# An adaLN-conditioned mixture-of-experts block on one core: loads, casts and splits at the start are put in another order

## What is computed

```python
# conditioning: one linear map plus a low-rank (rank 16) adapter chosen per sequence
A, Bm = lora_As[itok], lora_Bs[itok]                 # slot of each sequence, 32 slots
xt = x @ W.T + b + 2.0 * ((x @ A) @ Bm)
# router: 16 experts in 4 groups, 2 groups kept, 2 experts taken per token
scores = softmax(xt @ router_w + router_b) + router_bias
gate = top2_of_best_2_groups(scores)
# experts (512 -> 128 -> 512), and a shared expert (512 -> 256 -> 512)
y = sum_e gate[:, e] * ((silu(xt @ ew1[e] + eb1[e]) * (xt @ ew2[e] + eb2[e])) @ ew3[e] + eb3[e])
z = (silu(xt @ sw1 + sb1) * (xt @ sw2 + sb2)) @ sw3 + sb3
out = x + y + z
```

## Time and profile before

| | us |
|---|---|
| median of 3 runs | 132.3 |
| the runs | 130.42, 249.07, 132.3 |
| profiled execution | 131.28 |
| span of the profiled execution | 129.5 |

### The profile page before, as it was taken

The page is one execution under the profiler, slowest core; times in us unless marked ns, Lnnn a source line. Parts: engine busy times, 40 slices in busy tenths (PEclk is TensorE's granted clock), DMA queues, the critical chain, the costliest instruction groups (busy, mean ns, idle before and its releaser), DMA issues.

```text
span 129.5 us, 2241 instructions
## 1 busy us (share of the span) xinstructions
PE 123.5 (95%) x815; PEld 102.3 (79%) x815; DVE 86.0 (66%) x194; ACT 48.3 (37%) x85; POOL 19.8 (15%) x33
## 2 busy tenths in 40 slices
PE   6999996999996999999999999999999999999991
PEld 6988874987885777888888889987788888888891
DVE  1496095497469718989999984355906279997731
ACT  1780373595559516203963574441022110000000
POOL 7374025000000020000027200033620000000000
PEclk9999999999999999999999999999999999999999
DMA  4999888659999699989305899402426999422222
GB/s 102 375 287 347 259 331 273 225 199 370 317 301 309 140 178 175 321 305 358 123 0 116 321 309 384 161 11 83 162 86 209 328 369 375 179 97 109 110 94 81
DMA packets 16908, 28.77 MB, mean 222 GB/s; under 512 B 1952, under 2 KB 6432, under 8 KB 16768
## 3 DMA queue, kind: packets, MB, share of 16 engines
q1 hardware_dynamic: 11728, 17.07, 40.5%
q10 hardware_dynamic: 3952, 7.34, 16.5%
q0 software_dynamic: 1216, 4.20, 10.3%
HBM read 19.17 MB, written 9.44 MB: 221 GB/s over the span
## 4 chain that ended last, share of the span: by engine, by line
PE 77%; DMA 9%; DVE 5%; ACT 3%; issue 2%; SPq 2%; DVEq 0%; ACTq 0%
PE bank L993 58%; DMA xT_raw<-in_xT 9%; PE bank L1192 6%; PE bank L1206 3%; PE bank L1049 2%; ACT xT_h L462 2%; PE bank L1267 1%; PE bank L1060 1%; PE bank L1037 1%; PE bank L1182 1%; SPq L319 1%; DVE sw_l L682 1%; ACT loraA_sb L472 1%; PE bank L1023 1%; PE bank L1097 1%
## 5 line engine op out<-in xcount | busy, mean ns | idle before, releaser
L993 PE MATMUL bank<-xtT_h,sw_h 128*128 128x512 f32 x32 | 12.9, 405 | 1.2 <-DVE sw_l L682 1.2
L993 PE MATMUL bank<-xtT_h,w12e_h 128*128 128x512 f32 x32 | 13.1, 409 | 0.0
L993 PE MATMUL bank<-xtT_h,w12e_l 128*128 128x512 f32 x32 | 12.5, 391 | 0.0
L993 PE MATMUL bank<-xtT_l,w12e_h 128*128 128x512 f32 x32 | 12.5, 391 | 0.0
L993 PE MATMUL bank<-xtT_h,sw_l 128*128 128x512 f32 x32 | 12.5, 390 | 0.0
L993 PE MATMUL bank<-xtT_l,sw_h 128*128 128x512 f32 x32 | 12.5, 390 | 0.0
L966 DVE SCALAR_TENSOR_TENSOR x_sb<-rows_sb,val,x_sb 128x512 f32<-128x512 f32 x16 | 11.7, 748 | 0.2
L972 DVE TENSOR_TENSOR x_sb<-x_sb,bank 128x512 f32<-128x512 f32 (+1 forms) x9 | 5.6, 626 | 4.8 <-PE bank L993 4.8
L682 DVE TENSOR_TENSOR xT_l<-xT_raw,xT_h 128x512 fp32r<-128x512 f32 (+1 forms) x6 | 5.2, 867 | 4.5 <-ACT xT_h L462 4.5
L993 PEld LDWEIGHTS bank<-xtT_h,sw_h 128*128 128x128 f32 x32 | 6.0, 188 | 2.8 <-DVE sw_l L682 1.4
L790 DVE SCALAR_TENSOR_TENSOR heT_sb<-bank,b_dense,sg_sb 128x512 f32<-128x512 f32 x4 | 3.0, 751 | 7.7 <-PE bank L993 7.7
(11 more groups left out here) (184 smaller groups left out, 294.1 us busy)
## 6 DMA issues: line engine op xcount, KB each, us to landing
y_rows<-zeros ACTq DMA_DIRECT2D x2, 2048.0 KB, 12.2
rows_sb<-y_rows SPq DMA_DIRECT2D x8, 512.0 KB, 8.4
xT_raw<-in_xT SPq DMA_DIRECT2D x8, 256.0 KB, 5.8
xt_rows<-xt_turned SPq DMA_DIRECT2D x8, 256.0 KB, 8.1
x_sb<-in_x SPq DMA_DIRECT2D x1, 2048.0 KB, 11.2
w_ring<-in_w_turned SPq DMA_DIRECT2D x4, 512.0 KB, 9.0
out<-x_sb ACTq DMA_DIRECT2D x7, 256.0 KB, 2.0
condW_raw<-in_condWT ACTq DMA_DIRECT2D x4, 256.0 KB, 4.5
```

Of the source, the lines that this page charges most:

```text
L993: mm = pe.matmul(out, a[p], b[q], start=(start and n == 0), stop=(stop and n == 2))
```

## The change

x's second half is issued right behind the first, ahead of the six small loads, and the shared weights behind them without the wait for the second lora gather. VectorE casts the first chunk of x (a new semaphore, `first_hi`; the counts of `xT_hi` move by one). ScalarE does `copy_loraA(1)` ahead of `hi_lhT(0)`, both halves of `sw12` ahead of `hi_lhT(2)`, and `copy_loraA(3)` ahead of `hi_loraB(3)`. On VectorE the slot arithmetic comes behind the cast, both rests of x's second half come ahead of the lora rests, `lo_sw12(1)` comes ahead of `lo_lora(3)` and of the first choice, and the four transposes of the first half, which were interleaved with its rests, are done two by two: behind `lo_sw12(0)` and behind `choose(0)`. A wait for `xt_ready` stands before the transposes of the second half.

```diff
@@ -225,7 +225,7 @@
         xT_hi, xT_done, sw12_hi, sw12_done = sem("xT_hi"), sem("xT_done"), sem("sw12_hi"), sem("sw12_done")
         loraA_copied, xt_whole, loraB_hi, loraB_done = (
             sem("loraA_copied"), sem("xt_whole"), sem("loraB_hi"), sem("loraB_done"))
-        zeros_ready = sem("zeros_ready")
+        first_hi, zeros_ready = sem("first_hi"), sem("zeros_ready")
         lhT_hi, lhT_done, xtT_hi, xtT_done = sem("lhT_hi"), sem("lhT_done"), sem("xtT_hi"), sem("xtT_done")
         pool_step, consts_ready = sem("pool_step"), sem("consts_ready")
         lora_row_ready = sem("lora_row_ready")
@@ -322,16 +322,14 @@
             sp.dma_start(slot_i[:], seq_slot).then_inc(seq_in, 16)
             for k in range(1, KC):
                 load_xT(0, k)
+            for k in range(KC):
+                load_xT(1, k)
             sp.dma_start(condb_sb[:], cond_b).then_inc(small_in, 16)
             sp.dma_start(rw_sb[:], router_w).then_inc(small_in, 16)
             sp.dma_start(rb_col[:], router_b).then_inc(small_in, 16)
             sp.dma_start(rbias_sb[:], router_bias.partition_broadcast(P)).then_inc(small_in, 16)
             sp.dma_start(sb12_sb[:], sb12).then_inc(small_in, 16)
             sp.dma_start(b12_sb[:], b12).then_inc(small_in, 16)
-            sp.wait_ge(xT_in[KC - 1], 16)
-            for k in range(KC):
-                load_xT(1, k)
-            sp.wait_ge(lora_in[1], 16)
             sp.dma_start(sw12_raw[:], sw12).then_inc(sw12_in, 16)
             sp.dma_start(sw3_raw[:], sw3).then_inc(sw3_in, 16)
             sp.dma_start(b3s_raw[:], b3s).then_inc(b3s_in, 16)
@@ -509,14 +507,15 @@
                 act.dma_start(condW_raw[:, k, :], condWT[k]).then_inc(condW_in[k], 16)
             for k in range(KC):
                 hi_condW(k)
-                hi_xT(0, k, k + 1)
+                if k >= 1:
+                    hi_xT(0, k, k + 1)
             hi_xT(1, 0, 2)
+            hi_xT(1, 2, 4)
             hi_loraB(0)
             copy_loraA(0)
-            hi_xT(1, 2, 4)
             hi_loraB(1)
+            copy_loraA(1)
             hi_lhT(0)
-            copy_loraA(1)
             hi_lhT(1)
             act.wait_ge(small_in, 16 * 6)
             for m in range(KC):
@@ -530,13 +529,13 @@
             hi_loraB(2)
             copy_loraA(2)
             hi_sw12(0)
+            hi_sw12(1)
             hi_lhT(2)
-            hi_loraB(3)
             copy_lgT(0)
             copy_loraA(3)
+            hi_loraB(3)
             exps(0)
             hi_lhT(3)
-            hi_sw12(1)
             for m in range(KC):
                 whole_xtT(1, m)
             for m in range(KC):
@@ -672,11 +671,6 @@
             dve.wait_ge(consts_ready, 3)
             then(dve.tensor_scalar(part16_i[:], part_i[:], RANK - 1, None, ALU.bitwise_and))
             then(dve.tensor_copy(part16[:], part16_i[:]))
-            dve.wait_ge(seq_in, 16)
-            then(dve.tensor_copy(slot_f[:], slot_i[:]))
-            then(dve.tensor_scalar(slot_f2[:], slot_f[:], float(RANK), None, ALU.mult))
-            dve.tensor_scalar(lora_row[:], slot_f2[:], part16[:, 0:1], None, ALU.add).then_inc(lora_row_ready, 1)
-
             def rest(lo, whole, hi, made_sem):
 
                 dve.tensor_tensor(lo, whole, hi.bitcast(F32), ALU.subtract).then_inc(made_sem, 1)
@@ -687,7 +681,10 @@
 
             def lo_xT(n, first, last):
                 hi, lo = xT_split[n]
-                dve.wait_ge(xT_hi, last if n == 0 else KC + last // 2)
+                if n == 0 and first == 0:
+                    dve.wait_ge(first_hi, 1)
+                else:
+                    dve.wait_ge(xT_hi, first if n == 0 else KC - 1 + last // 2)
                 rest(lo[:, first:last], xT_raw[n][:, first:last], hi[:, first:last], xT_done)
 
             def lo_lora(g):
@@ -749,6 +746,12 @@
                                        cols_i[:, 0:E].unsqueeze(1).unsqueeze(1).to_broadcast(by_pick), ALU.is_equal))
                 dve.tensor_tensor(chosen[:, tiles], sel[:, 0, tiles], sel[:, 1, tiles], ALU.add).then_inc(chosen_ready, 1)
 
+            dve.wait_ge(xT_in[0], 16)
+            dve.tensor_copy(xT_split[0][0][:, 0, :], xT_raw[0][:, 0, :]).then_inc(first_hi, 1)
+            dve.wait_ge(seq_in, 16)
+            then(dve.tensor_copy(slot_f[:], slot_i[:]))
+            then(dve.tensor_scalar(slot_f2[:], slot_f[:], float(RANK), None, ALU.mult))
+            dve.tensor_scalar(lora_row[:], slot_f2[:], part16[:, 0:1], None, ALU.add).then_inc(lora_row_ready, 1)
             for k in range(KC):
                 lo_condW(k)
                 lo_xT(0, k, k + 1)
@@ -759,25 +762,29 @@
             then(dve.tensor_scalar(slot_no_pad[:], slot_no[:], float(K * T + T), None, ALU.add))
             then(dve.tensor_scalar(row_no[:], part_i[:], 63, None, ALU.bitwise_and))
             lo_xT(1, 0, 2)
+            lo_xT(1, 2, 4)
             lo_lora(0)
-            lo_xT(1, 2, 4)
             lo_lora(1)
             dve.wait_ge(consts_ready, 5)
             mask_lh(0)
             mask_lh(1)
             for m in range(KC):
-                turn_xt(0, m)
                 lo_xtT(0, m)
             lo_lora(2)
             lo_sw12(0)
+            turn_xt(0, 0)
+            turn_xt(0, 1)
             mask_lh(2)
+            lo_sw12(1)
             lo_lora(3)
             dve.wait_ge(small_in, 16 * 6)
             shift_logits(0)
             mask_lh(3)
             choose(0)
-            lo_sw12(1)
+            turn_xt(0, 2)
+            turn_xt(0, 3)
             dve.wait_ge(lgT_done, 1)
+            dve.wait_ge(xt_ready, KC)
             for m in range(KC):
                 turn_xt(1, m)
 
@@ -1002,7 +1009,10 @@
                         pe.matmul(cond_bank(0, m)[:], w[:, m * P:(m + 1) * P], x, start=start, stop=False)
 
                 pe.wait_ge(condW_hi, k + 1)
-                pe.wait_ge(xT_hi, k + 1)
+                if k == 0:
+                    pe.wait_ge(first_hi, 1)
+                else:
+                    pe.wait_ge(xT_hi, k)
                 over_dims(w_hi, x_hi, k == 0)
                 pe.wait_ge(condW_done, k + 1)
                 over_dims(w_lo, x_hi, False)
```

## The result

| | before | after |
|---|---|---|
| median of the runs timed together, us | 131.5 | 135.15 (134.28 to 135.75) |
| profiled execution, us | 131.28 | 135.57 |
| its span, us | 129.5 | 133.7 |

The changed kernel takes 1.030 times the time of the kernel before, 95% interval 1.017 to 1.043. The forecast was 131.9 with a range of 129.2 to 133.6, so the kernel is slower than forecast and outside the range.

What follows compares the result with a forecast made beforehand. TensorE, busy 95%, was taken as the bound. It gains 2.0 us by the shared experts, then stands 2.7 us for late dense weights; with + 0.6 net, 131.28 + 0.6 = 131.9 us, range 129.2 to 133.6.

Steps and rivals of the forecast that it cites:

- The early part: Up to the shared experts: waits of 1.1 and 1.2 us vanish, TensorE 2.0 us ahead; failing had 7%, 133.0 us.
- the new wait of 0.4 for the fourth mask's rest: Before the shared experts: TensorE, arriving earlier, waits about 0.4 us for VectorE's mask rest, between 0 and 0.7.
- VectorE's cast of x's first chunk: At the start: taken as 0.61 us from ScalarE's row, bounds nothing to twice that; gain 0.1 us, between 0 and 0.2.
- The step on x's second half: Loads at the start: issuing it early does not slow the first half and only frees VectorE, whose mask stood at 19.80.
- The queue: SP's queue before the dense experts: late stores delay the weights, TensorE stands 2.7 us, net + 0.6 us; 62%.
- The rival that they would run faster and the gain stay: First half's late stores: faster draining keeps the gain in whole or good part, 128.8 to 130.5 us; 18%.
- The rule of the Trainium skill, "DMA: Bandwidth & Descriptors", Specifications: Stores: 512-byte pieces suffice for line rate, so the 2.0 us gain would stay; the prediction preferred the trace's 184 GB/s.
- The rival of slower stores: Before the dense experts: eight stores drain under 160 GB/s, first weights land after 65.0, 133.9 us and up; 8%.
- The clock: After the 2.7 us standstill: TensorE falls to 1.2 GHz level, costing 2.0 us, 133.9 in all; a rival at 5%.
- the likeliest case: The dense weights' delay takes back the early gain, 130.8 to 133.2 us for 10% in the stores' rate; 62%.
- The late gather: Lora gathers come late beside the shared weights, early gains are lost, stores leave 1.1 us later: 133.0 us; 7%.
- The 3.9 us of slack: Second lora gather: landed at 14.21, turned at 18.07, so sharing DMA with the shared weights was priced at 0.

Runs made afterwards that it cites:

- E10: The changed kernel run again with nothing altered; 134.21 us, 1.026 times the kernel before.
- E8: E3 with x's second half issued behind the small loads, once the first half has landed, as before the change; 129.77 us, 0.992 times the kernel before.
- E2: The changed kernel, but SP again waits for the second lora gather before issuing the shared weights; 134.57 us, 1.032 times the kernel before.
- E4: The kernel before with only the first half's transposes moved late, plus the `xt_ready` wait; 135.75 us, 1.033 times the kernel before.
- E1: The changed kernel with the first half's four transposes put back between the splits; 128.86 us, 0.987 times the kernel before.
- E3: The changed kernel with transposes early again and shared weights again waiting for the second lora gather; 128.34 us, 0.982 times the kernel before.
- E6: The changed kernel, transposes still late, with x's 2 MB load moved behind the routed blocks' weights; 128.57 us, 0.985 times the kernel before.
- E7: E3 with x's 2 MB load moved behind the routed blocks' weights; 128.57 us, 0.981 times the kernel before.
- E9: E1 with the shared weights' loads issued ahead of the small loads; 128.94 us, 0.984 times the kernel before.
- E5: The changed kernel with six filler identity products on TensorE ahead of the dense weights' wait; median 133.33 us (131.82 to 134.51), no ratio.

## Why the prediction was wrong, by its own steps

**The early part: right, and a little small.** Both waits went. The terms of the sum were to come to 2.0 at the shared experts; in E10 the first shared matmul came at 39.67 against 42.04, so 2.4. The difference is the new wait of 0.4 for the fourth mask's rest, which none of the profiles shows: that term should have been 0. VectorE's cast of x's first chunk took 0.43 us (0.61 was taken). The step on x's second half was incomplete: "it only frees VectorE" overlooked ScalarE, whose first copy would otherwise stand behind that half's casts (E8, 1.2 to 1.4 us).

**The queue: right, nearly to the number.** The forecast beside E10, the execution without the late gather:

| step | forecast us | E10 us |
|---|---|---|
| stores of the first half issued | 41.4 | 41.24 |
| x landed | 61.75 | 50.02 + 11.5 = 61.5 |
| first dense weights cast (forecast: landed) | 63.05 | 62.89 |
| first dense matmul | 67.35 | 67.24 |
| standstill before it | 2.7 | 2.94 |

So the price of the late stores, taken from 184 GB/s in the earlier trace rows, held. The rival that they would run faster and the gain stay is answered by these times. The rule of the Trainium skill, "DMA: Bandwidth & Descriptors", Specifications, was set against that row; these runs bear the row out. The rival of slower stores is answered too: the weights came before 65.0 even in the profiled execution with the late gather (64.76).

**The clock: this step failed.** The prediction worked out a standstill of 2.7 us, said that none of that length is in the trace, and then went on as if the chip answered it like the ones of 1.1 and 1.2 that are there. It gave the other answer 5%, with a price of 2.0 us. Behind every standstill of 2.7 to 3.3 us that came without filling products (changed kernel, E2, E4, E10) the clock went to 0.50; the price was 1.7 us in three of them, 2.8 in E2. With the predicted 0.6 that makes 2.3, and 131.8 - 129.5 = 2.3 is what E10's span shows. These executions were no exceptions: in all 16 runs of the four kernels the mean granted clock was 0.974 to 0.987, in E1's four 0.998 or more. The prediction's own line for this case was 133.9; the medians are 134.2 and 135.15. The rule of the Trainium skill, "TensorE: Matmul & The Clock Gate", Part 1, that idleness sets the engine to half clock, stood beside that rival, and these traces agree with it (0.50). The chance was the error, not the mechanism: the likeliest case and this rival were one chain, since the first made the second's condition, and it should have been the likeliest or near it.

**The late gather: right as a rival, in one execution.** The 3.9 us of slack were exceeded in the first profile (second turn at 19.76, against 18.07 in the earlier trace rows), and the stores left at 42.92 instead of 41.24. The 1.9 us by which that span exceeds E10's are about this. How often the gather is late in runs without a profile can't be read, so it is not shown that it accounts for the 0.9 us between the two medians. The runs' mean clocks offer another reason: 0.974 or 0.975 in three of the first four, in one of E10's four, and that one took 1.1 us more than the mean of E10's others.

**The sum of it.** The change is two changes. All but the moved transposes make the kernel 1.3% faster (E1). The moved transposes cost 3.3% on the kernel before (E4), and on the changed one 1.026 / 0.987, or 4%, since they also take back the early start: TensorE arrives earlier and stands longer. E3, E6, E7 and E9 are, like E1, faster than both kernels, with intervals that overlap.

## What to carry to other kernels

Before a producer of stores is moved, list what stands behind these stores on the same queue up to the next load that the bottleneck engine waits for; here a load that nobody needed yet (x) made the stores' delay matter, and moving it cured the loss as well as moving the transposes back. When a forecast contains a standstill of the bottleneck engine longer than any in the trace, what the clock does after it is part of that same case and not a remote rival. Take apart a change of several parts by undoing the part that the price is on: the other parts here were worth having.

## What the runs showed of the hardware

- The granted clock fell about 1 us after TensorE resumed in the changed kernel (0.53 in 70 to 71, resumed at 69.11), but already before it resumed in E2 (0.81 in 65 to 66, resumed at 66.83). At 0.50 it stayed for six whole microseconds in E2 and for two or three elsewhere. Why E2's stretch is longer is open.
- With six small products ahead of the wait the clock stayed at 1.00 through a standstill of 2.16 us in E5's profiled execution, and in one more of its four runs; in the other two the mean clock was 0.987. The standstill of 0.81 in E3 had no visible effect (mean clock 0.998).
- The same gather landed 12.3 us after its issue in one execution of the changed kernel and 7.4 in the other (E10); with 1.5 MB of loads issued ahead of it, 10.1 (E9).
